# A normalised chunk turned by VectorE's 32x32 blocks and two transfers through memory instead of by TensorE

## What is computed

```python
x = x + _layernorm(attn(_layernorm(x)))   # x: 16 x 256 tokens x 256, causal, 16 heads of 128, biases
x = x + _layernorm(ffn(_layernorm(x)))    # 2048 wide, weights of 4 bits with a scale per 32
# attn: q, k, v = x W + b; softmax(mask(q k^T / sqrt(128))); z = attn v; out = z W_O + b_O
# ffn:  gate, up = x Wg, x Wu; inter = gelu(gate) * up; out = inter Wd
# _layernorm(x) = (x - mean) / sqrt(var + 1e-5)
```

## Time and profile before

| | |
|---|---|
| median of 3 runs | 1606.38 us (1605.19 to 1607.81) |
| the profiled execution | 1606.72 us, its span 1604.8 us |
| TensorE's granted clock | 0.998 of full on average |
| TensorE matmul busy | 1577.9 us, 98% |
| VectorE, ScalarE, GpSimd busy | 66%, 61%, 44% |
| DMA | 165.89 MB of the program's own, 32.8% of 16 engines' span |

### The profile page before, as it was taken

How to read it: one execution, slowest core, us unless ns; L and a number is a source line. 1 busy time by engine, 2 the same in 40 slices (tenths; PEclk the granted TensorE clock), 3 DMA queues, 4 the chain that set the end, 5 groups by cost and what they waited for, 6 DMA issues and landing times.

```text
span 1604.8 us, 28430 instructions
## 1 busy us (share of the span) xinstructions
PE 1577.9 (98%) x9600; PEld 1398.1 (87%) x9600; DVE 1060.9 (66%) x3074; ACT 975.6 (61%) x2433; POOL 711.6 (44%) x1069
## 2 busy tenths in 40 slices
PE   6999999999999999999999999999999999999998
PEld 5888899889888988888889888888888888888887
DVE  4666677677767677677767766665656556565665
ACT  5887677767776777677767766644444444444443
POOL 5764455445554455455445533333333333333333
PEclk9999999999999999999999999999999999999999
DMA  4653434434443444443444455561000010000000
GB/s 122 186 172 116 129 128 149 142 116 142 149 139 119 142 142 137 127 151 126 142 128 136 142 157 162 155 214 40 27 14 27 14 40 27 14 28 14 27 15 25
DMA packets 157440, 167.69 MB, mean 104 GB/s; under 512 B 15856, under 2 KB 130672, under 8 KB 157296
## 3 DMA queue, kind: packets, MB, share of 16 engines
q1 hardware_dynamic: 157296, 165.89, 32.8%
HBM read 94.53 MB, written 71.30 MB: 103 GB/s over the span
## 4 chain that ended last, share of the span: by engine, by line
PE 85%; DMA 6%; ACT 3%; DVE 2%; SPq 2%; issue 1%; POOL 1%; DVEq 0%; POOLq 0%
PE fbank L692 14%; PE fbank L694 14%; PE fbank L693 14%; PE obank L694 7%; PE obank L693 7%; PE obank L692 7%; PE ubank L692 5%; PE ubank L693 5%; PE ubank L694 5%; PE ubank L716 3%; DMA turned_scratch<-turned 3%; PE fbank L794 3%; DMA back<-turned_scratch 2%; SPq L494 2%; ACT probs L589 1%
## 5 line engine op out<-in xcount | busy, mean ns | idle before, releaser
L692 PE MATMUL fbank<-xnT_hi,weights 128*128 128x512 f32 x768 | 305.8, 398 | 1.1 <-DVE xnT_lo L870 1.1
L693 PE MATMUL fbank<-xnT_lo,weights 128*128 128x512 f32 x768 | 304.7, 397 | 0.0
L694 PE MATMUL fbank<-xnT_hi,weights 128*128 128x512 f32 x768 | 304.6, 397 | 0.0
L1238 POOL TENSOR_TENSOR pT_lo<-back,pT_hi 128x512 fp32r<-128x512 f32 x128 | 165.9, 1296 | 284.9 <-ACT pT_hi L654 284.9
L600 ACT ACTIVATE w_raw<-fbank 128x512 f32<-128x512 f32 x128 | 76.4, 597 | 262.7 <-PE fbank L694 262.7
L1200 POOL TENSOR_SCALAR probs<-probs,rsum 128x128 f32<-128x128 f32 (+1 forms) x512 | 208.9, 427 | 20.6 <-DVE rsum L893 16.7
L694 PEld LDWEIGHTS fbank<-xnT_hi,weights 128*128 128x128 f32 x768 | 145.1, 189 | 35.2
L885 DVE CUSTOM_DVE_ANT_0 probs<-ubank,mask 128x128 f32<-128x128 f32 (+1 forms) x512 | 155.0, 355 | 29.1 <-PE ubank L694 28.3
L692 PEld LDWEIGHTS fbank<-xnT_hi,weights 128*128 128x128 f32 x768 | 145.2, 189 | 27.0 <-DVE xnT_lo L870 1.5
L693 PEld LDWEIGHTS fbank<-xnT_lo,weights 128*128 128x128 f32 x768 | 145.2, 189 | 24.7
L974 DVE SCALAR_TENSOR_TENSOR w_raw<-w_raw,fbank 128x512 f32<-128x512 f32 x128 | 87.9, 687 | 113.3 <-ACT w_raw L600 113.3
(11 more groups left out here) (122 smaller groups left out, 4571.9 us busy)
## 6 DMA issues: line engine op xcount, KB each, us to landing
turned_scratch<-turned SPq DMA_DIRECT2D x128, 384.0 KB, 2.6
back<-turned_scratch SPq DMA_DIRECT2D x512, 96.0 KB, 2.2
w_raw<-in_w_pairs SPq DMA_DIRECT2D x32, 256.0 KB, 3.3
w_hi_scratch<-w_hi SPq DMA_DIRECT2D x48, 128.0 KB, 2.0
w_lo_scratch<-w SPq DMA_DIRECT2D x48, 128.0 KB, 2.0
weights<-w_hi_scratch SPq DMA_DIRECT2D x24, 256.0 KB, 3.6
weights<-w_lo_scratch SPq DMA_DIRECT2D x24, 256.0 KB, 4.1
x_res<-in_x SPq DMA_DIRECT2D x16, 256.0 KB, 2.9
```

The lines of the kernel that those rows point to most:

```text
L692: nc.tensor.matmul(out, a[0], b[0], start=start, stop=False, skip_group_check=skip)
L693: nc.tensor.matmul(out, a[0], b[1], start=False, stop=False, skip_group_check=skip)
L694: return nc.tensor.matmul(out, a[1], b[0], start=False, stop=stop, skip_group_check=skip)
L1238: pool.tensor_tensor(lo[:].rearrange("p u b (a j) -> p (u b) a j", j=32), mem.back[m % 2][:, :, 0:2].rearrange("p a u b j -> p (u b) a j") ...
```

## The change

Both "xT" jobs and their banks go. VectorE turns each normalised chunk in 32x32 blocks (`turn_rows`), SyncE writes the blocks to memory in one transfer of 512 KB (`send_rows`) and reads them back in four of 128 KB into `x_in` (`fetch_rows`), and a new job "rows" splits them into `xnT` (ScalarE `rows_hi`, VectorE `rows_lo`). In the attention stage the norm moves from steps 10, 12 and 13 to the ends of steps 1 and 5 and is done in place; the blocks are turned in steps 10 and 12, sent in 12 and fetched in 13. The input of a chunk is loaded in step 15 of the one before (chunk 1's right at the start), the residual in steps 1 and 3. In the first chunk two of the four v jobs move from step 0 to step 1. In the MLP the turning is the fifth piece of the norm (tile 11), and the turned rows go alternately to `xnT` and to `zT` and `pT` as a second buffer.

```diff
-X1_ROOTS, NEXT_ROOTS = 6, 13
+X1_ROOTS, NEXT_ROOTS = 6, 3
...
-        return [("q", 1), ("k", 1), ("scores", 0), *values, ("T", 0), ("scores", 1)]
+        return [("q", 1), ("k", 1), ("scores", 0), *values[:2], ("T", 0), ("scores", 1)]
+    if n == 1:
+        return [("q", 2), ("k", 2), *values[2:], ("T", 1), ("pT", 0), ("scores", 2)]
     plan = [("q", n + 1), ("k", n + 1), ("T", n)]
     if n % HEADS == HEADS - 2:
-        plan += [("xT", 0)]
+        plan.insert(2, ("rows", n // HEADS + 1))
...
+    def send_rows(n):
+        sp.wait_ge(s.rows_turned, 2 * n + 2)
+        if n:
+            sp.wait_ge(s.rows_back, 64 * n)
+        sp.dma_start(rows_v.rearrange("a i k c -> (a i) k c"),
+                     mem.turned_at(n).rearrange("p k t r i -> p k (t r i)")
+                     ).then_inc(s.rows_sent, 16)
+
+    def fetch_rows(n):
+        sp.wait_ge(s.rows_sent, 16 * (n + 1))
+        for k in range(4):
+            sp.dma_start(mem.rows_back[32 * k:32 * k + 32].rearrange("p a t r i -> p a (t r i)"),
+                         rows_v[:, :, k].rearrange("a i c -> i a c")).then_inc(s.rows_back, 16)
...
+        if j == 13:
+            fetch_rows(c)
...
+        elif j == 12:
+            send_rows(c)
         elif j == 15:
-            load_res(c, 0)
-            if c == NCH - 1:
-                load_res(c, 1)
-        elif c and j == 1:
-            load_res(c - 1, 1)
+            for i in range(2):
+                if c < NCH - 1:
+                    next_x(c + 1, i)
+                else:
+                    load_res(c, i)
+        elif c and j in (1, 3):
+            load_res(c - 1, (j - 1) // 2)
...
+    def turn_rows(n, t):
+        for i in (t, t + 1):
+            last = dve.transpose(mem.turned_at(n)[:, :, i].rearrange("p k r i -> p r k i"),
+                                 x_in[:, i, :].rearrange("p (k j r) -> p r k j", r=KT, j=BLK))
+        last.then_inc(s.rows_turned, 1)
+
+    def rows_lo(n, dst):
+        for kt in range(KT):
+            dve.wait_ge(s.rows_hi, KT * n + kt + 1)
...
-    NEXT_AT = {(10, "sum"): (0,), (12, "sum"): (1, 2), (13, "end"): (3, 4)}
+    NEXT_AT = {(1, "end"): (0, 1, 2), (5, "end"): (3, 4), (10, "sum"): (5,), (12, "sum"): (6,)}
```

More of the change, by code:

```diff
@@ L244, in __init__ @@
         self.turned = sb("turned", [P, 4, 3, 2, 32])
-        self.back = [sb(f"back{i}", [P, 4, 3, 2, 32]) for i in range(2)]
+        backs = sb("back", [P, 2, 4, 3, 2, 32])
+        self.back = [backs[:, i] for i in range(2)]
         self.zT = [sb(f"zT_{s}", [P, CHUNK], F32R) for s in ("hi", "lo")]
@@ L269, in __init__, with blocks @@
                                                             for i in range(2))]
+        def blocks(view):
+            return view.rearrange("p (k t r i) -> p k t r i", t=TT, r=KT, i=BLK)
+        self.rows_turned = [blocks(self.stream[:].rearrange("p t d -> p (t d)")), blocks(raw),
+                            blocks(backs[:].rearrange("p n a u b j -> p (n a u b j)")[:, 0:TT * D])]
+        self.rows_back = blocks(self.x_in[:].rearrange("p t d -> p (t d)"))
+        self.rows = [[[p[:, kt, :] for kt in range(KT)] for p in self.xnT],
+                     [[p[:] for p in self.zT],
+                      [p[:].rearrange("p u b q -> p (u b q)") for p in self.pT]]]
         def bank(name, shape):
@@ L556, in load_program @@
         finish_y(c)
+        if c < NCH - 1:
+            send_rows(NCH + c)
+            fetch_rows(NCH + c)
     for i in range(2):
@@ L649, in scalar_program @@
                 full(count, mem.zT[0][:], bank, mem.bias_v[:, h:h + 1]).then_inc(s.hi, 1)
-            else:
-                full(count, mem.xnT[0][:, m, :], bank).then_inc(s.hi, 1)
+        elif kind == "rows":
+            rows_hi(m - 1, mem.rows[0])
         elif kind == "pT":
@@ L669, in scalar_program @@
         n = c * NT + m
-        if kind == "xT":
-            for kt in range(KT):
-                act.wait_ge(s.xT, c * KT + kt + 1)
-                act.activation(mem.xnT[0][:, kt, :], (mem.gbank, mem.hbank)[kt][0][:],
-                               ACT.Copy).then_inc(s.xT_hi, 1)
+        if kind == "rows":
+            rows_hi(NCH + c, mem.rows[m % 2])
         elif kind == "gu":
@@ L707, in project @@
         last.then_inc(s.full, 1)
-    def transpose_x(src, kt, bank):
-        for t in range(TT):
-            last = nc.tensor.transpose(bank[:, t * P:(t + 1) * P], src[:, t, kt:D:KT], mem.ident[:])
-        return last
     def scores(u, i, b):
@@ L759, in tensor_program @@
             if kind == "q" and h == 0:
-                pe.wait_ge(s.lo, split(("xT", m // HEADS, KT - 1)))
+                pe.wait_ge(s.rows_lo, KT * (m // HEADS))
             project(bank, h, 0 if kind == "q" else 1)
-        elif kind == "xT":
-            if m == 0:
-                pe.wait_ge(s.xn, c + 1)
-            transpose_x(mem.stream, m, bank).then_inc(s.full, 1)
         elif kind == "v":
@@ L813, in tensor_program @@
             if m == 0:
-                pe.wait_ge(s.lo, split(("xT", NCH, KT - 1)))
+                pe.wait_ge(s.rows_lo, KT * NCH)
             if m < 2:
@@ L933, in norm_next_x @@
             moments()
[L934 to L940 removed]
+        elif part in (3, 4):
+            dve.wait_ge(s.rstd, next_norm(c))
+            after(standardise(x_in, x_in, 2 * (part - 3)))
+        else:
+            if part == 5 and c == 1:
+                dve.wait_ge(s.w_split, len(PAIRS))
+            elif part == 5 and c:
+                dve.wait_ge(s.rows_sent, 16 * c)
+            turn_rows(c, 2 * (part - 5))
     def spread(n):
@@ L1035, in vector_program @@
                     extra(c, j, "sum")
-            else:
-                full(count, mem.xnT[1][:, m, :], mem.xnT[0][:, m, :], bank)
+        elif kind == "rows":
+            rows_lo(m - 1, mem.rows[0])
         elif kind == "T":
@@ L1100, in norm_next_y @@
             dve.wait_ge(s.rstd, y_next_norm(c))
-            last = standardise(x_in, x_in, 2 * (part - 2))
-            if part == 3:
-                last.then_inc(s.xn, 1)
+            after(standardise(x_in, x_in, 2 * (part - 2)))
+        else:
+            if c:
+                dve.wait_ge(s.rows_sent, 16 * (NCH + c))
+            for t in (0, 2):
+                turn_rows(NCH + c, t)
     def between(c, j):
@@ L1112, in vector_program @@
         n = c * NT + m
-        if kind == "xT":
-            for kt in range(KT):
-                dve.wait_ge(s.xT_hi, c * KT + kt + 1)
-                dve.tensor_tensor(mem.xnT[1][:, kt, :], (mem.gbank, mem.hbank)[kt][0][:],
-                                  mem.xnT[0][:, kt, :].bitcast(F32),
-                                  ALU.subtract).then_inc(s.xT_lo, 1)
+        if kind == "rows":
+            rows_lo(NCH + c, mem.rows[m % 2])
         elif kind == "gu":
```

84 lines of the change are left out of this document (42 added, 42 removed).

## The result

The changed kernel is slower: median 1623.08 us (1618.53 to 1628.36, 4 runs) against 1605.85 us before; the ratio is 1.0106, 95% interval 1.0074 to 1.0139. The forecast was 1610.8, with 1619.0 as its upper end. The profiled execution took 1623.76 us, 17.0 more than that of before.

What follows compares the result with a forecast made beforehand. TensorE, busy 98% of the span, was taken as the bound. Minus 2.2, 0.8 and 0.9, plus 2.8, 1.0, 1.5 and 3.0 made plus 4.4: 1611.1, or 1610.8 us against the median; range 1600.5 to 1619.

Steps and rivals of the forecast that it cites:

- TensorE's removed work: Transposes leave TensorE's queue: 0.94 us per attention chunk, 7.5 for eight, and 6.65 in the MLP, together 14.2.
- The MLP boundary: At MLP chunk changes xnT_lo keeps its place on VectorE; TensorE gains 0.1 us each, 0.8 for seven.
- The attention boundary: At attention chunk changes the VectorE and ScalarE chain takes back 5.3 of 7.5 us removed; gain 2.2.
- The loads: 512 KB of input in step 15 delay fetched probabilities once more in each of seven chunks: plus 1.5 us.
- The late rows: Fetched rows land near 391.4 to 392.4, needed at 391.8, at attention boundaries: plus 1.0 us in all.
- the sign to look for: ScalarE's rows_hi was to wait under 1 us for its data.
- The end of step 5: Four normalising operations delay kT_lo by 1.0 us; scores wait 0.46 in each of six chunks: plus 2.8 us.
- The start: In the first chunk "T" of head 1 starts near 36.0, 3.8 us late; cost plus 3.0 us.
- Chunk 7's stall stays: Chunk 7's stall of 3.46 us, behind other transfers, was to remain.
- the three rivals: Chains give way, 1599.6 us, chance 0.2; turned rows land late, 1617.8, chance 0.2; start costs nothing, 1607.8, chance 0.15.
- The nearest, late rows: Turned rows land 1 us later than taken at each of seven attention boundaries: 1617.8 us, chance 0.2.
- The third: Two fewer v jobs in step 0 offset the statistics, so the start costs nothing: 1607.8 us, chance 0.15.

Runs made afterwards that it cites:

- experiment 4: Changed kernel with the attention rows turned in steps 6 and 8, sent in 10 and fetched in 12, instead of 10, 12, 12 and 13: ratio 1.0099.
- experiments 1 and 2: Changed kernel with MLP rows turned in tile 9 instead of 11: ratio 1.0044; the second also splits them in tile 12 instead of 13: 1.0025.
- Experiment 7: Changed kernel with the rows' split behind the transposes of the probabilities ("T") in step 14 instead of ahead of them: ratio 1.0049.
- 5 and 6: Changed kernel, input halves loaded in steps 15 and 1, residual in 3 and 5: ratio 1.0119; kernel before, both residual halves in step 15: 1.0006.
- experiment 3: Changed kernel with two normalising pieces moved from the end of step 5 to the sums of step 4: ratio 1.0070.
- Experiment 11: Changed kernel with "T" first, normalising in step 4, MLP rows turned in tile 9, split in 12, v jobs back in step 0, statistics in step 2: 0.9963.
- a3: The kernel of experiment 4: changed kernel with the attention rows turned, sent and fetched earlier; ratio 1.0099.
- a2: Changed kernel with the input's halves loaded in steps 15 and 1 and the residual's in steps 3 and 5: ratio 1.0119.
- a5: The kernel of Experiment 7: changed kernel with "T" ahead of the rows' split in step 14; ratio 1.0049.
- c2: The kernel of Experiment 11: changed kernel with three edits and all four v jobs back in step 0; ratio 0.9963.

## Why the prediction was wrong

- **TensorE's removed work: right.** The stretch 14 to 15 shrinks by 0.97 to 1.14 at four of the changed kernel's first seven boundaries, by 0.67 at one, and by 1.82 and 1.47 at two, where the waits for the store went too; 0.94 was forecast.
- **The MLP boundary: the step that failed.** The prediction said "Its place on VectorE ... stays. So TensorE gains 0.2 to 0.3". I never timed the rows' trip here: I counted 1.4 us for the turning in tile 11 and took its result as ready. It takes 6.9 us from turned to landed and ends at 1128.8, and TensorE then waits 1.3 to 1.7 us seven times. -0.8 was forecast and 7.3 measured. Some 3 of the 7.3 are the rows of the last attention chunk, for which the MLP's first matmul waits 1.8 at 1053.61, a place for which the prediction had no term; experiment 4, which has these rows in time, takes 2.8 away. The other 4 or so are the seven boundaries, and experiments 1 and 2 take their waits away.
- **The attention boundary: the sum was right for the path I priced, and the wrong path.** I argued that "the same 2.4 us lie between kT_lo and the masks", and that held (2.37). But the order also moves "T", which starts 1.1 to 2.6 us behind kT_lo's end, and behind "T" lie its send, its fetch and ScalarE's pT_hi. That path had no term. Experiment 7 gives it 9 us by the ratio and 5 to 10 by the stretches; by the estimate there 5.1 of it remain when the rows are in time, and the rest, up to 4, would be late rows that hold "T" up still further. With "T" first the stretch 15 to 3 loses 3.3, where the priced chain had 5.3. The loads, at 1.5, were not the cause: 5 and 6 gain nothing. The late rows, at 1.0, were sized low: TensorE waits 0.96, 0.54 and 0.86 for xnT_lo at three of seven attention boundaries, and ScalarE's rows_hi waits up to 1.19 there, 2.45 in chunk 7 and 1.4 to 1.7 in the MLP, where under 1 was the sign to look for. But having them early (4) gains only 1 us, since the wait moves.
- **The end of step 5: right.** 2.8 forecast, 3.1 in the six chunks by experiment 3, since the wait of 0.45 is followed by 0.12 in the next step.
- **The start: the chain right, the cost wrong, the number near by luck.** "T" of head 1 stands at 36.15, and the scores behind it wait. But this costs nothing that lasts: in the two profiles with the changed start and the full clock, head 14 comes 0.5 and 0.6 earlier than before, and in six more it comes 1.1 to 5.5 later, in the order of the time at the lower clock. The average over the eight is 2.1, where 3.0 was forecast, so the term was about right for a reason that it did not name. Experiment 11 shows no gain by undoing the start.
- **"Chunk 7's stall stays": wrong, in the other direction.** It is gone in the changed kernel, where that chunk's 14 to 15 shrinks by 6.1 us and 0.8 was counted. With the new boundary it is at most 0.15 us long in six of ten kernels, and 1.75, 0.92, 0.68 and 1.76 us in a3, a2, a5 and c2; the stretch shrinks by 4.2 to 6.1. A part of this is chance in the first profile of before, whose stall was the longest of four: against the other three the 6.1 are 3.4 to 5.1. Why the probabilities' transfer of step 124 is less late there was not tried.

None of the three rivals was it. The nearest, late rows, was right at the MLP, where I had not put it; at the attention boundary, where I had, it was a part that could not be gained by itself. The third, a start that costs nothing, is what the profiles at full clock show.

So 17 us instead of 4.4: 8 more from the MLP, 5 from the stretch 15 to 3 ("T" and late rows, less what the chain was priced too high), some 2 each from the start of that execution (its clock), the end of step 5 with chunk 7's share, and the steps 8 to 14 (0.7 to 1.1 in most kernels with the same order), less 6 from the stall and smaller things.

## What to carry to other kernels

When work moves from a busy engine to a path through memory, time the whole trip, from the operation that makes the data to the landing of the last piece, and start it early enough; "it is made in time" is not "it is there in time". When a job changes places with another on an idle engine, follow everything that each of the two releases, not only the next thing on that engine: here the job that slipped fed a loop of send, fetch and split that had 1.6 us in hand, and two moves together took 2.3. Look at the granted clock before a difference at the start is put down to the order of work. And a removal that frees 14 us may need three moves around it before 5 to 6 of them show.
